# A graph network's tables in three bfloat16 parts: who casts and who subtracts between the neighbour sums

## The chip, the cores and the metric

The kernel runs on one core of a Trainium2 chip. A core has five engines with instruction streams of their own: TensorE (PE in the profile; its weight loads are PEld), VectorE (DVE), ScalarE (ACT), GpSimd (POOL) and SyncE (SP). They meet only through semaphores, and SP, ACT and POOL can also start DMA transfers. The metric is the device time of the whole program in microseconds (us), and lower is better.

## The reference

Four graph blocks run in sequence on 6250 nodes with 96 features and 200000 edges. The first is an attention layer, the second two layers with a maximum over neighbours, the third two layers with a mean (MEAN1, MEAN2 here), the fourth three graph convolutions (GCN1 to GCN3). Each block's result is added to its input and normalised. What the change touches are the sums over neighbours of the last two blocks:

```python
def _sage_layer(h, src, dst, W_l, b_l, W_r):
    msgs = h[src]
    agg = jax.ops.segment_sum(msgs, dst, num_segments=N_NODES)
    ...
    return mean @ W_l + b_l + h @ W_r
...
def gcn_conv(x, W, b, src, dst, deg_inv_sqrt):
    h = x @ W
    msgs = h[src] * norm[:, None]
    out = jax.ops.segment_sum(msgs, dst, num_segments=N)
    out = out + h * (deg_inv_sqrt * deg_inv_sqrt)[:, None]
    return out + b
```

## The kernel before

Nodes lie in 49 blocks of 128 partitions (NB), which are handled in 7 groups of 7 blocks (NG, GB). In the three earlier passes over the edges the kernel gathers rows edge by edge. In the second and third of these it also builds, in device memory, a matrix of counts: how many edges lead from each node to each other, as bfloat16. The five sums (n = 0 for MEAN1, 1 for MEAN2, 2 to 4 for GCN1 to GCN3) are then dense matrix products of this matrix with the table of the layer's rows.

The count matrix is read anew for each sum, in 49 blocks of 1568 KB. `load_blocks` (L413 to L430) loads each block in two halves of 784 KB: SP loads one, ACT the other, each from its own instruction stream. Three blocks fit in the buffer (CNT16 in BUF), so a block may be loaded as soon as the sum of the block three places earlier is done (`sums_ready`). SP has nothing else to do and reaches the next sum's loads as soon as there is room. ACT reaches them when it has done everything that stands ahead of them in its stream (L1121 to L1128): the node phase of that sum.

To keep float32 accuracy the table TBW (in TB) is split into three bfloat16 parts that stand side by side in PARTS (in CG): the first part is the table cast to bfloat16; the rest is the table minus the first part, and goes to EGW (in EG); the second part is the rest cast; the third is the rest minus the second part. TensorE's block sum (L719 to L741) makes 49 matrix products of a 128x128 piece of counts with 288 columns of PARTS, accumulated in one of three PSUM banks (psA, psB, psX), and VectorE takes each block from there (`take_block`, L1686 on). The first block of a sum waits at every seventh product for that group's parts (`parts_made`, L734).

Between two sums lies a node phase that makes the new table, group by group, over all engines:

- TensorE transposes 7 blocks of rows into psX (L671), and multiplies the transposed rows by the layer's weights into psO (L679). It transposes group g + 1 ahead of multiplying group g. psO holds one group, and is free again at `out_used`.
- ACT copies psX to XTQ (`rows_transposed`, L900), one copy per group. In MEAN2 it also copies the other half of psO to R (`root_rows`, L905, shown as ARENA) and gives psO back. In GCN1 to GCN3 VectorE gives it back.
- VectorE takes the table out of psO (`take_rows`: L1247 in MEAN2, L1244 in the GCNs, shown as TB), casts the first part (L1215) and subtracts (L1216), both in `split`, L1211.
- GpSimd casts the second part (L486) and subtracts for the third (L489), in the loop `second_and_third_parts` (L481), once for each sum.

Each engine's order is written out by hand; nothing is scheduled by a planner.

Of the kernel before, what the change touches and what calls it, by code (L numbers as in the profile page):

```python
# [8 lines left out]
DIM = 96  # L9
# [6 lines left out]
GB = 7  # L16
NG = NB // GB
# [44 lines left out]
ALU = mybir.AluOpType  # L62
# [4 lines left out]
ATT, PROJ, MAX1, MAX2, MEAN1, MEAN2, GCN1, GCN2, GCN3 = range(9)  # L67
PHASE_COLS = [W0 + HEADS, DIM] + [2 * DIM] * 4 + [DIM] * 3

PASS_OF_PHASE = {ATT: 0, MAX1: 1, MAX2: 2, MEAN1: 3, MEAN2: 4, GCN1: 5, GCN2: 6, GCN3: 7}  # L70
GATHER_PASSES = 3
MAX_PASSES = (1, 2)


EARLY, LATE = slice(0, NB - GB), slice(NB - GB, NB)
# [27 lines left out]
def build(nc, x, src, dst, dst_before, src_tiles, dst_tiles, edge_attr, att_W, att_src, att_dst, gat_bias, proj_WT, proj_b, ln_g, ln_b,  # L103
# [7 lines left out]
    def sem(name):  # L111
        return ctx.enter_context(nc.semaphore(name))
# [25 lines left out]
    TBW = TB[:, 0:NB * DIM].rearrange("p (b w) -> p b w", w=DIM)  # L138
    EG = sb("EG", [P, NB * W0])
    EG0 = EG[:, :].rearrange("p (b w) -> p b w", w=W0)  # L140
    EGW = EG[:, 0:NB * DIM].rearrange("p (b w) -> p b w", w=DIM)
# [34 lines left out]
    PARTS = CG[:, 0:NB * 3 * DIM // 2].bitcast(BF16).rearrange("p (b w) -> p b w", w=3 * DIM)  # L176
# [122 lines left out]
    table_made = sem("table_made")  # L299
# [54 lines left out]
    again_taken = sem("again_taken")  # L354
    again_step = sem("again_step")
    large_known = sem("large_known")
    rest_made = sem("rest_made")
    second_made = sem("second_made")
    parts_made = sem("parts_made")
# [75 lines left out]
    def _(pool):  # L435
# [12 lines left out]
        for b in range(NB):  # L448
            g, j = b // GB, b % GB
# [31 lines left out]
        def second_and_third_parts(n):  # L481
            with pool.Fori(0, NG) as g:
                here = bass.ds(g * GB, GB)
                pool.wait_ge(rest_made, g + (n * NG + 1))
                pool.sem_inc(turn["pool"], 1)
                nc.gpsimd.tensor_copy(PARTS[:, here, DIM:2 * DIM], EGW[:, here, :]).then_inc(second_made, 1)  # L486
                pool.wait_ge(second_made, g + (n * NG + 1))
                pool.sem_inc(turn["pool"], 1)
                nc.gpsimd.tensor_tensor(PARTS[:, here, 2 * DIM:3 * DIM], EGW[:, here, :], PARTS[:, here, DIM:2 * DIM],  # L489
                                        ALU.subtract).then_inc(parts_made, 1)  # L490
# [11 lines left out]
        for q in range(GATHER_PASSES):  # L502
# [10 lines left out]
            if q == 0:  # L513
                pool.wait_ge(step_row_stored, 16)
            if q in MAX_PASSES:
                for j in range(CS):
# [4 lines left out]
                    in_offset=bass.IndirectOffsetOnAxis(ap=last_i[:, b:b + 1], axis=0)).then_inc(end_gathered[b // GB], 16)  # L521

        second_and_third_parts(0)

        for n in range(1, 8 - GATHER_PASSES):
            second_and_third_parts(n)

    @block.sync
    def _(sp):
# [360 lines left out]
    def _(act):  # L890
# [11 lines left out]
        def root_rows(f, g):  # L902

            act.wait_ge(table_made, PASS_OF_PHASE[f] * NG + g + 1)
            nc.scalar.copy(R[:, g * GB:(g + 1) * GB, :], OUTG[:, :, DIM:2 * DIM]).then_inc(out_used, 1)  # L905

        def node_phase(f, first=0):

            for g in range(first, NG):
                rows_transposed(f, g)  # L910
                if g and f in (MAX1, MAX2, MEAN1, MEAN2):
                    root_rows(f, g - 1)
            if f in (MAX1, MAX2, MEAN1, MEAN2):
                root_rows(f, NG - 1)

        def attention_pass():

# [182 lines left out]
        for f in (MAX1, MAX2, MEAN1, MEAN2, GCN1, GCN2, GCN3):  # L1100
# [14 lines left out]
            else:  # L1115
                n = PASS_OF_PHASE[f] - GATHER_PASSES
# [16 lines left out]
    def _(dve):  # L1133
        steps = [0, 0]

        def link(ins, behind=0):


            steps[0] += 1
            ins.then_inc(dve_step, 1)  # L1140
            dve.wait_ge(dve_step, steps[1] + (steps[0] - behind))
# [7 lines left out]
        tt = nc.vector.tensor_tensor  # L1149
# [61 lines left out]
        def split(here, g):  # L1211


            rest = EGW[:, here, :]
            link(nc.vector.tensor_copy(PARTS[:, here, 0:DIM], TBW[:, here, :]))  # L1215
            link(tt(rest, TBW[:, here, :], PARTS[:, here, 0:DIM], ALU.subtract))  # L1216
            dve.sem_inc(rest_made, 1)  # L1217
# [20 lines left out]
        def take_rows(f, g):  # L1238

            here = slice(g * GB, (g + 1) * GB)  # L1240
            dve.wait_ge(out_ready, g + (out_group_base(f, "rows") + 1))
            if f in PASS_OF_PHASE:
                if f in (GCN1, GCN2, GCN3):
                    tt(TBW[:, here, :], OUTG[:, :, 0:DIM], dis[:, here].unsqueeze(2).broadcast_to([P, GB, DIM]),  # L1244
                       ALU.mult).then_inc(table_made, 1)
                else:
                    ts(TBW[:, here, :], OUTG[:, :, 0:DIM], 1.0, None, ALU.mult).then_inc(table_made, 1)  # L1247
                if f in (MAX1, MAX2):
                    return
                dve.wait_ge(table_made, g + (PASS_OF_PHASE[f] * NG + 1))  # L1250
                if f in (GCN1, GCN2, GCN3):
                    dve.sem_inc(out_used, 1)
                split(here, g)

        def node_rows(f):

            for g in range(NG):
                take_rows(f, g)
            rows_taken(f)

        def rows_taken(f):
            if f in PASS_OF_PHASE:
                dve.wait_ge(table_made, (PASS_OF_PHASE[f] + 1) * NG)
            dve.wait_ge(out_used, out_group_base(f, "rows") + NG + 1)
# [5 lines left out]
        for g in range(NG):  # L1270
            here = slice(g * GB, (g + 1) * GB)
# [515 lines left out]
        for g in range(NG):  # L1787
            here = slice(g * GB, (g + 1) * GB)
# [26 lines left out]
        for g in range(NG):  # L1815
            here = slice(g * GB, (g + 1) * GB)
# [82 lines left out]
```

## Time and profile before

| | us |
|---|---|
| median of 3 runs | 8144.81 |
| the runs | 8144.05 to 8150.12 |
| the profiled execution | 8149.13 |
| its span on the core | 8147.2 |

The profile is of one execution. The first 6811 us of the span are the attention and maximum layers and MEAN1. The rest is four stretches of one kind: a node phase, then 49 block sums of some 6 us. MEAN2's node phase begins at 6811 us, GCN1's at 7151, GCN2's at 7481 and GCN3's at 7811.

### The profile page before, as it was taken

What the parts mean: (1) busy time and instruction counts of PE and PEld (TensorE: products, weight loads), DVE (VectorE), ACT (ScalarE), POOL (GpSimd) and SP (SyncE); (2) the same over time, 40 slices, a digit from 0 to 9 for tenths busy, and PEclk for the clock granted to TensorE, in tenths of its full rate; (3) what the DMA queues carried; (4) which work ended last, traced back from release to release, by engine and by line L of the source; (5) the groups of instructions that cost most, each with busy time, mean ns of one, the idle gap of its engine ahead of it and who ended that gap; (6) DMA issues with size and microseconds to landing.
All of it is one profiled execution on the core that took longest, in us unless ns stands there. A gap on an engine that the chain in (4) does not pass through costs nothing.

```text
span 8147.2 us, 70764 instructions
## 1 busy us (share of the span) xinstructions
PE 4234.8 (52%) x19184; PEld 2471.1 (30%) x19184; DVE 5020.9 (62%) x9411; ACT 2884.7 (35%) x5375; POOL 4827.2 (59%) x5030
## 2 busy tenths in 40 slices
PE   2110000000255555666665566566566598999999
PEld 1000000000131111111113111111111398999999
DVE  4654444444568888888786778878887774222232
ACT  0222222222255555555553555555555300010000
POOL 6777777777637777777776777777777500000000
PEclk6555555555565555555555555555555599999999
DMA  5333333333224444444443444444444275766767
GB/s 132 88 98 85 85 87 87 85 85 85 66 86 131 130 131 133 132 131 133 133 131 101 133 131 131 133 133 131 131 133 132 84 268 199 267 223 220 267 228 248
DMA packets 642166, 1129.68 MB, mean 139 GB/s; under 512 B 164844, under 2 KB 422271, under 8 KB 641618
## 3 DMA queue, kind: packets, MB, share of 16 engines
q1 hardware_dynamic: 360112, 437.17, 17.2%
q0 software_dynamic: 159184, 251.10, 14.8%
q10 hardware_dynamic: 122578, 438.40, 13.6%
q14 instruction: 216, 1.77, 0.1%
q8 instruction: 76, 1.25, 0.1%
HBM read 713.46 MB, written 412.70 MB: 138 GB/s over the span
## 4 chain that ended last, share of the span: by engine, by line
POOL 48%; PE 21%; issue 17%; DVE 10%; DMA 4%; ACT 1%; DVEq 0%; POOLq 0%; SPq 0%; ACTq 0%
POOL CG L460 46%; PE psX L736 6%; PE psB L736 6%; PE psA L736 6%; DMA CG<-table,BUF 3%; DVE BUF L1550 2%; PE psO L679 1%; DVE XTQ L1576 1%; DVE BUF L1545 1%; DVE STG L1576 1%; DVE BUF L1542 1%; DVE XTQ L1569 1%; DVE STG L1569 1%; ACT X L1045 1%; POOL EG L519 1%
## 5 line engine op out<-in xcount | busy, mean ns | idle before, releaser
L460 POOL DMA_INDIRECT CG<-table,BUF x4704 | 4482.0, 953 | 1567.5 <-issue 1351.7
L706 PE MATMUL psO<-WE,BUF 128*128 128x384 f32 x1568 | 1141.7, 883 | 381.7 <-DMA BUF<-in_edge_attr 381.7
L1001 ACT ACTIVATE BUF<-iota,EG 128x128 bf16<-128x128 f16 x3136 | 958.0, 387 | 205.1 <-ACT CG L981 103.0
L779 PE MATMUL psA<-ident,F 128*100 128x128 f32 x1 | 0.5, 455 | 1704.3 <-DVEq L1451 1704.3
L486 POOL CAST CG<-EG x35 | 26.9, 769 | 1296.1 <-DVEq L1217 1296.1
L977 ACT COPY psX<-BUF 128x384 f32<-128x384 f32 x392 | 189.0, 482 | 1540.0 <-DVE XTQ L1576 771.0
L706 PEld LDWEIGHTS psO<-WE,BUF 128*128 128x128 f32 x1568 | 459.6, 323 | 893.8 <-DMA BUF<-in_edge_attr 646.5
L1542 DVE TENSOR_SCALAR BUF<-iota,EG 128x392 bf16<-128x392 f16 x1568 | 562.1, 358 | 46.9 <-DMA EG<-step_rows 19.1
L1480 DVE TENSOR_TENSOR terms<-CG,ARENA 128x64 f32<-128x64 f32 x98 | 26.3, 269 | 904.2 <-DMA CG<-table,BUF 903.7
L1545 DVE TENSOR_SCALAR BUF<-iota,EG 128x392 bf16<-128x392 f16 x1568 | 543.4, 347 | 6.5 <-PE psB L716 3.3
L779 PEld LDWEIGHTS psA<-ident,F 128*100 128x100 f32 x1 | 0.2, 162 | 1704.7 <-DVEq L1451 1704.7
L1569 DVE TENSOR_TENSOR XTQ<-CG,psO 128x768 f32<-128x768 f32 x196 | 288.2, 1470 | 366.6 <-DMA CG<-table,BUF 366.6
L736 PE MATMUL psA<-CG,BUF 128*128 128x288 bf16 x4018 | 509.3, 287 | 6.4 <-DMA BUF<-counts 6.1
L736 PE MATMUL psB<-CG,BUF 128*128 128x288 bf16 x4018 | 508.7, 287 | 7.2 <-DMA BUF<-counts 6.9
L1569 DVE TENSOR_TENSOR STG<-CG,psO 128x768 f32<-128x768 f32 x196 | 288.4, 1471 | 355.4 <-DMA CG<-table,BUF 355.4
L736 PE MATMUL psX<-CG,BUF 128*128 128x288 bf16 x3969 | 500.9, 286 | 0.5 <-POOL CG L489 0.5
L736 PEld LDWEIGHTS psB<-CG,BUF 128*128 128x128 bf16 x4018 | 494.8, 142 | 9.7 <-issue 7.2
L736 PEld LDWEIGHTS psA<-CG,BUF 128*128 128x128 bf16 x4018 | 494.9, 142 | 9.2 <-POOL CG L489 7.0
L736 PEld LDWEIGHTS psX<-CG,BUF 128*128 128x128 bf16 x3969 | 488.3, 142 | 1.6 <-POOL CG L489 0.8
L715 PE MATMUL psA<-BUF 128*128 128x392 bf16 x523 | 250.4, 479 | 405.1 <-DVE BUF L1545 396.3
L715 PE MATMUL psB<-BUF 128*128 128x392 bf16 x523 | 250.1, 478 | 401.8 <-DVE BUF L1545 393.0
L1005 ACT ACTIVATE BUF<-BUF,ones 128x1024 bf16<-128x1024 bf16 x392 | 449.7, 1147 | 12.7
(284 smaller groups left out, 7533.6 us busy)
## 6 DMA issues: line engine op xcount, KB each, us to landing
BUF<-counts SPq DMA_DIRECT2D x245, 784.0 KB, 5.8
BUF<-counts ACTq DMA_DIRECT2D x245, 784.0 KB, 6.4
counts<-BUF SPq DMA_DIRECT2D x1572, 98.0 KB, 2.3
hist<-CG ACTq DMA_DIRECT2D x392, 384.0 KB, 2.4
hist<-CG ACTq DMA_DIRECT2D x196, 416.0 KB, 2.5
CG<-table,BUF POOLq DMA_INDIRECT x4704, 2.5
BUF<-in_edge_attr SPq DMA_DIRECT2D x392, 128.0 KB, 3.3
table<-TB SPq DMA_DIRECT2D x14, 336.0 KB, 2.6
```

The source lines that it names most:

```text
L460: pool.indirect_dma_start(out=rows_in[:, u % RING, k, :], out_offset=None, in_=tab, in_offset=bass.IndirectOffsetOnAxis(ap=SRC[:, u * S + ...
L706: mm = pe.matmul(ETERM[:, s, a, 0:4 * DIM], EA[:, s, a, :], WE[:, m, :, :].rearrange("k c d -> k (c d)"), start=True, stop=True)
L715: pe.matmul(sums, LOW[:, s, j, 0, :], RHS[:, j, 0, :], start=True, stop=False)
L736: mm = pe.matmul(sums[:, 0:3 * DIM], CNT16[:, B % 3, b:b + NB * (P - 1) + 1:NB], PARTS[:, b, :], start=b == 0, stop=b == NB - 1, skip_grou ...
L977: nc.scalar.copy(reset_cols[:, :, 1:K9], reset[:, u * S:(u + 1) * S].unsqueeze(1).broadcast_to([P, DIM // 2, S])).then_inc(resets_ready, 1)
L1001: far = nc.scalar.activation(FAR[:, j, a, :], iota16[:, 0:P], ACT.Square, bias=STEP[:, 2 + a, u * CS + j:u * CS + j + 1], scale=-1.0)
L1005: nc.scalar.activation(LOW[:, u % 2, :, :, :], FAR, ACT.Relu, bias=ones[:, 0:1], scale=-1.0).then_inc(low_ready, 1)
L1542: ts(RHS[:, j, 0, :], iota16[:, :], STEP[:, 0, n:n + 1], None, ALU.is_equal)
L1545: ts(RHS[:, j, 1, :], iota16[:, :], STEP[:, 1, n:n + 1], None, ALU.is_equal).then_inc(onehot_ready, 1)
L1550: stt(ACC[:, j, :], ACC[:, (j - 1) % CS, :], STEP[:, 4, n:n + 1], step_sums[k % 3], ALU.mult, ALU.add).then_inc(acc_ready, 1)
L1569: tt(max_cols[b][:, :, 1:K9].rearrange("p c (a k) -> p c a k", a=2), ROWSW[:, r, :, :].rearrange("p (a k) c -> p c a k", a=2), ETERM[:, s, ...
L1576: scan = nc.vector.tensor_tensor_scan(out=columns, data0=reset_flat, data1=columns, initial=0.0, op0=ALU.add, op1=ALU.max)
```

## The change

In MEAN2, GCN1, GCN2 and GCN3 (`SPLIT_HERE`) ACT now makes the first and the second part, and VectorE both subtractions. ACT's new casts stand one and two groups behind its copies out of psX; VectorE's second subtraction stands one group behind its first. GpSimd's loop runs only for MEAN1, whose split stays as it was. A new semaphore, `first_made`, tells VectorE of a finished first part, and VectorE waits at the end of the node phase until all parts are made.

```diff
@@ -521,9 +523,6 @@
         second_and_third_parts(0)
-
-        for n in range(1, 8 - GATHER_PASSES):
-            second_and_third_parts(n)
@@ -910,8 +909,28 @@
                 rows_transposed(f, g)
                 if g and f in (MAX1, MAX2, MEAN1, MEAN2):
                     root_rows(f, g - 1)
+                if g and f in SPLIT_HERE:
+                    if g >= 2:
+                        second_part(f, g - 2)
+                    first_part(f, g - 1)
             if f in (MAX1, MAX2, MEAN1, MEAN2):
                 root_rows(f, NG - 1)
+            if f in SPLIT_HERE:
+                second_part(f, NG - 2)
+                first_part(f, NG - 1)
+                second_part(f, NG - 1)
+
+        def first_part(f, g):
+            here = slice(g * GB, (g + 1) * GB)
+            act.wait_ge(table_made, PASS_OF_PHASE[f] * NG + g + 1)
+            nc.scalar.copy(PARTS[:, here, 0:DIM], TBW[:, here, :]).then_inc(first_made, 1)
+
+        def second_part(f, g):
+            here = slice(g * GB, (g + 1) * GB)
+            act.wait_ge(rest_made, (PASS_OF_PHASE[f] - GATHER_PASSES) * NG + g + 1)
+            nc.scalar.copy(PARTS[:, here, DIM:2 * DIM], EGW[:, here, :]).then_inc(second_made, 1)
@@ -1250,12 +1269,34 @@
-                split(here, g)
+                if f in SPLIT_HERE:
+                    if g:
+                        third_part(f, g - 1)
+                    rest_of_first(f, g)
+                else:
+                    split(here, g)
+
+        def rest_of_first(f, g):
+            here = slice(g * GB, (g + 1) * GB)
+            dve.wait_ge(first_made, SPLIT_HERE.index(f) * NG + g + 1)
+            link(tt(EGW[:, here, :], TBW[:, here, :], PARTS[:, here, 0:DIM], ALU.subtract))
+            dve.sem_inc(rest_made, 1)
+
+        def third_part(f, g):
+            here = slice(g * GB, (g + 1) * GB)
+            dve.wait_ge(second_made, (PASS_OF_PHASE[f] - GATHER_PASSES) * NG + g + 1)
+            tt(PARTS[:, here, 2 * DIM:3 * DIM], EGW[:, here, :], PARTS[:, here, DIM:2 * DIM],
+               ALU.subtract).then_inc(parts_made, 1)
         def node_rows(f):
             for g in range(NG):
                 take_rows(f, g)
+            if f in SPLIT_HERE:
+                third_part(f, NG - 1)
+                dve.wait_ge(parts_made, (PASS_OF_PHASE[f] - GATHER_PASSES + 1) * NG)
             rows_taken(f)
```

ACT's stream from GCN2's node phase to its first load of counts reads so before (XTQ is the transposed rows; TENSOR_LOAD large reads the flag that picks the branch with the loads):

```order
L900 COPY XTQ<-psX 96x896 [waits transposed] x2
L900 COPY XTQ<-psX 96x896 [waits out_ready,transposed] x5
L1124 TENSOR_LOAD large
L1124 ISA x2
L1125 COMPARE_AND_BRANCH
L429 UNCONDITIONAL_BRANCH
L429 ISA
L426 ISA [waits sums_ready]
```

The same place in the changed kernel, from the last copy of transposed rows on (CG is PARTS, TB the table, EG the rest; line numbers are those of the changed kernel):

```order
L899 COPY XTQ<-psX 96x896 [waits out_ready,transposed]
L933 CAST CG<-EG 128x7x96 [waits rest_made]
L927 CAST CG<-TB 128x7x96 [waits table_made]
L933 CAST CG<-EG 128x7x96 [waits rest_made]
L927 CAST CG<-TB 128x7x96 [waits table_made]
L933 CAST CG<-EG 128x7x96 [waits rest_made]
L1143 TENSOR_LOAD large
L1143 ISA x2
L1144 COMPARE_AND_BRANCH
L431 UNCONDITIONAL_BRANCH
L431 ISA
L428 ISA [waits sums_ready]
```

Five casts, each with a wait on VectorE, stand now between ACT's last copy and its first load of counts.

VectorE's stream at the end of GCN2's node phase reads so before (the last group and the first block taken):

```order
L1244 TENSOR_TENSOR TB<-psO,dis 128x672 [waits dve_step,out_ready]
L1215 CAST CG<-TB 128x7x96 [waits table_made]
L1216 TENSOR_TENSOR EG<-TB,CG 128x672 [waits dve_step]
L1686 TENSOR_REDUCE EG<-psA 128x96 [waits dve_step,sums_ready,out_used,table_made]
L1676 TENSOR_TENSOR EG<-EG,TB 128x96 [waits sums_used]
```

And in the changed kernel:

```order
L1263 TENSOR_TENSOR TB<-psO,dis 128x672 [waits dve_step,out_ready]
L1290 TENSOR_TENSOR CG<-EG,CG 128x7x96 [waits table_made,second_made]
L1283 TENSOR_TENSOR EG<-TB,CG 128x672 [waits first_made]
L1290 TENSOR_TENSOR CG<-EG,CG 128x7x96 [waits dve_step,second_made]
L1727 TENSOR_REDUCE EG<-psA 128x96 [waits out_used,sums_ready,table_made,parts_made]
```

The cast is gone from VectorE's stream, and a second subtraction stands in it that waits for ACT.

## Rows read from the trace of the kernel before

**Rows 1.** Page, part 1: busy us (share of span) and instructions of each engine.

```profile
PE 4234.8 (52%) x19184; PEld 2471.1 (30%) x19184; DVE 5020.9 (62%) x9411; ACT 2884.7 (35%) x5375; POOL 4827.2 (59%) x5030
```

**Rows 2.** Windows, inside GCN2's sum: length; PE, PEld, DVE, ACT, POOL; clock, DMA, GB/s.

```profile
7527.00:7790.00 263.00, 263.00 (x2149) 263.00 (x2148) 54.71 (x176) 0.00 (x0) 0.00 (x0) 1.00 0.75 267
```

**Rows 3.** Chain that ended last, MEAN2's node phase to its sum: start, us, what.

```profile
6847.90 0.87 DVE TB L1247
6848.79 0.49 ACT ARENA L905
...
6849.31 0.18 ACTq L1124
...
6850.00 4.59 DMA BUF<-counts
```

**Rows 4.** Timeline, MEAN2: start, us, engine, line, operation [idle before <-releaser].

```profile
6842.80 0.72 ACT L905 COPY ARENA<-psO 128x672 f32<-128x672 f32 x1 [2.78 <-DVE TB L1247]
...
6854.72 7.66 PE L736 MATMUL psB<-CG,BUF 128*128 128x288 bf16 x49 [6.86 <-DMA BUF<-counts]
...
6862.22 6.17 PE L736 MATMUL psX<-CG,BUF 128*128 128x288 bf16 x49
```

**Rows 5.** Timeline of GCN2's node phase and the start of its sum.

```profile
7498.68 0.86 DVE L1216 TENSOR_TENSOR EG<-TB,CG 128x672 f32<-128x672 f32 x1
...
7499.69 0.86 DVE L1244 TENSOR_TENSOR TB<-psO,dis 128x672 f32<-128x672 f32 x1
...
7500.75 1.77 PE L679 MATMUL psO<-WR,XTQ 96*128 96x96 f32 x14 [0.36 <-DVEq L1252]
7500.96 1.46 POOL L489 TENSOR_TENSOR CG<-EG,CG  x1 [0.27 <-POOL CG L486]
7501.58 1.56 DVE L1216 TENSOR_TENSOR EG<-TB,CG 128x672 f32<-128x672 f32 x1
...
7503.28 0.86 DVE L1244 TENSOR_TENSOR TB<-psO,dis 128x672 f32<-128x672 f32 x1
...
7506.92 0.90 ACT L900 COPY XTQ<-psX 96x896 f32<-96x896 f32 x1 [2.69 <-PE psX L671]
...
7507.93 32.23 ACTq L426 DMA_DIRECT2D BUF<-counts  x7
...
7514.06 0.86 DVE L1244 TENSOR_TENSOR TB<-psO,dis 128x672 f32<-128x672 f32 x1
...
7521.37 6.17 PE L736 MATMUL psB<-CG,BUF 128*128 128x288 bf16 x49
```

**Rows 6.** Chain that ended last, end of GCN2's node phase: start, us, what.

```profile
7518.94 1.47 POOL CG L489
...
7520.45 1.08 PE psA L736 x7
```

**Rows 7.** Tile counts, ACT's first load of GCN2's sum (issued at 7507.93).

```profile
DMA to landing us min/median/max: 4.5/4.5/4.5
```

**Rows 8.** Timeline of GCN1: tables taken out of psO, second block's start.

```profile
7172.54 0.86 DVE L1244 TENSOR_TENSOR TB<-psO,dis 128x672 f32<-128x672 f32 x1
...
7183.52 0.86 DVE L1244 TENSOR_TENSOR TB<-psO,dis 128x672 f32<-128x672 f32 x1
...
7190.95 6.17 PE L736 MATMUL psA<-CG,BUF 128*128 128x288 bf16 x49
```

**Rows 9.** Timeline of GCN3: the same three places.

```profile
7824.24 0.86 DVE L1244 TENSOR_TENSOR TB<-psO,dis 128x672 f32<-128x672 f32 x1
...
7838.62 0.86 DVE L1244 TENSOR_TENSOR TB<-psO,dis 128x672 f32<-128x672 f32 x1
...
7845.93 6.17 PE L736 MATMUL psX<-CG,BUF 128*128 128x288 bf16 x49
```

**Rows 10.** Groups by line and form, ACT: count, busy us, mean ns, idle before them.

```profile
L981 ACT COPY CG<-STG 128x768 f32<-128x768 f32 x196 | 307.3, 1568 | 0.0
...
L905 ACT COPY ARENA<-psO 128x672 f32<-128x672 f32 x28 | 20.1, 717 | 83.2 <-DVE TB L1247 83.2
```

More of the change, by code:

```diff
@@ L72 @@
 MAX_PASSES = (1, 2)
+SPLIT_HERE = (MEAN2, GCN1, GCN2, GCN3)
 EARLY, LATE = slice(0, NB - GB), slice(NB - GB, NB)
@@ L356, in build @@
     large_known = sem("large_known")
+    first_made = sem("first_made")
     rest_made = sem("rest_made")
```

## The prediction

> **What bounds the kernel now.** I read the page first. GpSimd is busy for 59% of the span and VectorE for 62% [rows 1], but almost all of that lies in the first 6811 us, which the change doesn't touch. So I read the last 1336 us only, by windows. Inside a sum TensorE is busy for all of the 263 us of the window, at full clock, with DMA at 0.75 of its engines' time [rows 2]: the sums are TensorE's, a block in 6.0 us, and nothing that starts late is made up later, since TensorE has no idle time there to give back. What can change are the four node phases in between, from the last block of one sum to the second block of the next, where TensorE waits for others.
>
> Then I asked the chain of waits who ends a node phase. In MEAN2 it is not the split. The last table group is taken at 6847.90, ACT copies its half of psO, reads the flag, starts its first load of counts at 6850.00, and this transfer takes 4.59 us [rows 3]. TensorE had been idle for 6.86 us when it came [rows 4]. In GCN2 ACT's first load leaves at 7507.93, while the node phase still runs, and lands 4.5 us later [rows 5, 7], so at 7512.4, ahead of TensorE's first block. There the end is the split: VectorE's three operations per group, then GpSimd's subtraction, then the last seven products of block 0 [rows 6]. GCN1 and GCN3 look the same.
>
> **Part 1: VectorE is rid of a collision.** While GpSimd subtracts for 1.46 us (from 7500.96), VectorE's own subtraction takes 1.56 us instead of 0.86 [rows 5]. I checked the period of a GCN group: from one table taken to the next it is 7503.28 - 7499.69 = 3.59 us with the collision, 3.66 in GCN1, as (7183.52 - 7172.54)/3 [rows 5, 8]. Without it VectorE's three operations are 3 x 0.86 plus some 0.35 of gaps, 2.9 us; and the round through psO is the product's 1.77 us, the table's 0.86 and two handings over (the product started 0.2 us after the table was done, and TensorE's end reaches VectorE in about 0.2), 3.0 us. So a group costs 3.0 instead of 3.6. Until the third table nothing is gained: there the products are longer, and VectorE waits for them. From there to the last table: GCN2 has four periods, (7514.06 - 7499.69) - 12.0 = 2.4 us; GCN3 (7838.62 - 7824.24) - 12.0 = 2.4 us [rows 9]; GCN1 from the fourth table on has three, (7183.52 - 7172.54) - 9.0 = 2.0 us. In MEAN2 the product is longer, ACT sits idle for 2.78 us a group [rows 4] and its two new casts of about 0.6 us of occupancy each fit there: no gain, no loss.
>
> The Trainium skill weighs in on the size of this: the page "SBUF — State Buffer", section "Who interferes with whom", says that a VectorE operation with two SBUF inputs is held until a reading GpSimd operation has ended. By that rule the held subtraction would end 0.86 us after 7502.42, so at 7503.28; the trace ends it at 7503.14, and the row agrees within 0.14. The gain would be the same 0.7 us a group by either.
>
> **Part 2: the casts on ACT.** ACT gets 14 casts of 128x672 a phase. The trace of before has none from SBUF to bfloat16 of that form. The nearest row is L905, the same number of elements out of PSUM: 0.717 us [rows 10]. The far bound above is L981, which reads with a stride: 1568/768 = 2.04 ns an element, so 1.37 us for 672. I take 0.72, because the cast's inner runs are 96 contiguous elements on both sides, as L905's nearly are. A cheaper one than 0.6 I exclude, as its elements are no fewer.
>
> **Part 3: what is queued behind them.** This is the term that decides. ACT's first three loads of counts stand behind its last cast, and the last cast waits for VectorE. Let t be the start of the last table group. In a GCN: table done t + 0.86; first part of group 6 by ACT to t + 1.6; VectorE has meanwhile done the third part of group 5 (to t + 1.9), then the rest of group 6 to t + 2.75; with 0.15 for the semaphore the last cast starts at t + 2.9. From the start of a copy of this form to the DMA's issue MEAN2 shows 6850.00 - 6848.79 = 1.2 us [rows 3] (GCN2 1.0, from 7506.92 to 7507.93 [rows 5]). So the load leaves at t + 4.1 and TensorE starts block 0 after 4.6 + 0.1 us, at t + 8.8. Before, the load left 6.1 us ahead of t; that is a delay of 10 us for the load, of which the split's old tail covered a part.
>
> Block 0 then follows an idle TensorE. MEAN2's block 0, after 6.86 us of idling, took 6862.22 - 6854.72 = 7.5 us to the next block's start instead of 6.0 [rows 4]; I take this for all four. So the second block starts at t + 16.3.
>
> Before it started at t + 7.4 in GCN1 (7190.95 - 7183.52) and t + 7.3 in GCN2 and GCN3 (7521.37 - 7514.06; 7845.93 - 7838.62) [rows 5, 8, 9]. The loss is 8.9, 9.0 and 9.0 us; less the gain of part 1 it is 6.9, 6.6 and 6.6.
>
> In MEAN2 t doesn't move. ACT does its copy of psO from t + 0.9, the second part of group 5 from 1.5, the first of group 6 from 2.1 to 2.85; VectorE the third part of 5 from 2.25 to 3.1, the rest of 6 to 4.0; the last cast starts at t + 4.15, the load leaves at t + 5.35 instead of t + 2.1. Loss 3.25 us, and block 0 is as slow as it was.
>
> The Trainium skill has a rule against such an order, in "DMA: Bandwidth & Descriptors", section "Rules for kernel authors": issue a DMA early, compute, and wait late, so that its fixed cost lies under the work. The trace agrees on the cost of the other order (MEAN2's 6.86 us of waiting [rows 4]); by that rule each of the three GCN loads goes from hidden to paid.
>
> **Part 4: at nothing.** Splitting ends sooner (last third part at about t + 4.5, before 7520.4, t + 6.3), but that is now under the transfer, worth nothing. GpSimd's 56 operations leave a queue that nobody else used. VectorE's wait for all parts ends before the first block's sum comes. SP's halves are issued as before.
>
> **The sum:** 3.25 + 6.9 + 6.6 + 6.6 = 23.4 us slower. Against the profiled execution's 8149.1 that is 8172.5; the median of the runs is 4.3 us lower, so 8144.8 + 23.4 = 8168.2 us.
>
> **The rivals.**
>
> A: the load doesn't wait. If ACT's stream reached its DMA ahead of the casts' ends, or block 0 waited for something else, the loads would land as before and the split's tail would decide: block 0 would start when the last product ends, run into group 6's parts at t + 4.5, which is before it needs them, and only part 1's gain would count, 2.0 + 2.4 + 2.4 = 6.8 us faster: 8138, within 0.2% of before, so not slower. It decides at one point: in a GCN the load must have left by about t - 2, which it did at t - 6.1 before. Against it speaks MEAN2, where the load left 1.2 us after the last copy's start and TensorE waited for it. 6%.
>
> B: the casts are slow, at 1.37 us. Then ACT's 0.9 + 2 x 1.37 us make a GCN group 3.7 us, the gain of part 1 is gone (6.8 us), two casts on a GCN's tail add 1.3 us each phase and MEAN2 gets 2 us at the tail and 1 in its groups: 23.4 + 6.8 + 3.9 + 3 = 37, 8182. 8%.
>
> C: the clock stays low for longer after 8 to 10 us of idling than after MEAN2's 6.86. At the worst all of block 0 runs at half clock, 12.0 us instead of 7.5 in four phases: 8168 + 18 = 8186. 6%.
>
> D: the loads are late but cost less: the transfer lands sooner on a quiet machine, and the clock is back sooner (6.0 for block 0). 1.5 us in each GCN and 1 us of issue and landing in all four take 8.5 off: 8160, within 0.2%. 10%.
>
> **How the numbers follow.** My forecast, 8163 to 8174 around 8168, has 70%. A measurement of this kernel tells about 0.2% (16 us, so 8161.1) from no change. Slower: forecast, B, C, and nothing of D, 0.84, from which I take a little for errors on the low side: 0.82. Same: A, D and that little, 0.17. Faster by over 16 us has no mechanism: 0.01. The range leaves out A below and C above: 8156 to 8180, down past D and up to short of B.
>
> **What would show it.** In the trace after: ACT's first load of counts some 4 us behind the last table in GCN1 to GCN3, and 5.3 in MEAN2; TensorE idle for 8 to 9 us ahead of block 0, released by DMA of counts, not by the third part; VectorE's subtractions all at 0.86; a GCN group at 3.0 us; casts on ACT of 0.7 to 0.8. It is wrong if ACT's loads leave before the last cast, if the third part releases block 0, or if TensorE's blocks inside a sum are not 6.0 us.

## The result

| | before | after |
|---|---|---|
| median, us | 8148.05 | 8174.01 |
| runs, side by side on one chip | 8 (8144.05 to 8152.92) | 8 (8167.39 to 8176.02) |
| profiled execution, us | 8149.13 | 8174.0 |
| its span, us | 8147.2 | 8172.1 |

The ratio of after to before is 1.003, with a 95% interval of 1.0021 to 1.0039. The change costs 26.0 us; the prediction had 23.4.

The page's first part says little, as it said before [rows 1]: GpSimd has 58 us less to do, ACT 39 us more, and the program is longer.

```profile
PE 4226.2 (52%) x19184; PEld 2469.9 (30%) x19184; DVE 5009.8 (61%) x9411; ACT 2924.1 (36%) x5431; POOL 4769.2 (58%) x4974
```

The groups by line show the new operations. First ACT's casts from 6811 us on, for the rest and for the table (count | busy us, mean ns | idle ahead and what ended it); then VectorE's two subtractions from 7157 us on.

```profile
L933 ACT CAST CG<-EG 128x672 bf16<-128x672 f32 x28 | 21.1, 753 | 11.5 <-DVEq L1284 11.5
L927 ACT CAST CG<-TB 128x672 bf16<-128x672 f32 x28 | 21.1, 753 | 18.7 <-DVE TB L1263 18.7
...
L1290 DVE TENSOR_TENSOR CG<-EG,CG 128x672 bf16<-128x672 f32 x21 | 18.0, 857 | 5.3 <-ACT CG L933 2.6
L1283 DVE TENSOR_TENSOR EG<-TB,CG 128x672 f32<-128x672 f32 x21 | 17.9, 851 | 2.5 <-ACT CG L927 2.5
```

A cast takes 0.75 us, and no subtraction is stretched any more: their means are 0.85 us, where a stretched one took 1.56 [rows 5]. So each of the moved operations is cheap, and the loss is elsewhere. The chain that ended last, in MEAN2 (answering to [rows 3]), shows where:

```profile
6853.81 0.49 ACT CG L933
6854.33 0.18 ACTq L1143
...
6855.02 4.74 DMA BUF<-counts
...
6859.89 7.68 PE psB L735 x49
```

The last cast, then the reading of the flag, then the load, then block 0. The timeline of the same place (answering to [rows 4]):

```profile
6849.72 0.86 DVE L1266 TENSOR_SCALAR TB<-psO 128x672 f32<-128x672 f32 x1 [1.99 <-PE psO L678]
...
6859.89 7.68 PE L735 MATMUL psB<-CG,BUF 128*128 128x288 bf16 x49 [10.21 <-DMA BUF<-counts]
...
6867.41 4.82 PE L735 MATMUL psX<-CG,BUF 128*128 128x288 bf16 x38
```

TensorE idles 10.21 us ahead of block 0, where it idled 6.86 before. In GCN1 the wait is new (answering to [rows 8]):

```profile
7183.32 0.86 DVE L1263 TENSOR_TENSOR TB<-psO,dis 128x672 f32<-128x672 f32 x1 [0.24 <-PE psO L678]
...
7186.20 0.86 DVE L1263 TENSOR_TENSOR TB<-psO,dis 128x672 f32<-128x672 f32 x1 [0.24 <-PE psO L678]
...
7188.92 0.75 ACT L933 CAST CG<-EG 128x672 bf16<-128x672 f32 x1 [1.08 <-DVEq L1284]
...
7189.93 24.79 ACTq L428 DMA_DIRECT2D BUF<-counts  x6
...
7194.44 7.66 PE L735 MATMUL psX<-CG,BUF 128*128 128x288 bf16 x49 [8.28 <-DMA BUF<-counts]
...
7201.93 6.17 PE L735 MATMUL psA<-CG,BUF 128*128 128x288 bf16 x49
```

A group now takes 7186.20 - 7183.32 = 2.88 us, and everything after the last table is later. TensorE's waits from 6800 us on list all four places (sum in us, times, longest; psB stands for two of them):

```profile
PE psB L735 <- DMA BUF<-counts: 18.6, 2, 10.2
...
PE psA L735 <- DMA BUF<-counts: 8.5, 1, 8.5
...
PE psX L735 <- DMA BUF<-counts: 8.3, 1, 8.3
```

To compare kernels I use one measure, read off each timeline: a **phase** runs from the first transposes of a node phase to the start of the second block of its sum. The **last stretch** runs from MEAN2's first transposes to the end of the span.

| us | MEAN2 | GCN1 | GCN2 | GCN3 | sum | last stretch |
|---|---|---|---|---|---|---|
| before | 50.9 | 39.3 | 40.5 | 34.7 | 165.4 | 1335.9 |
| after | 54.3 | 44.6 | 50.5 | 38.6 | 187.9 | 1358.9 |
| difference | +3.4 | +5.3 | +10.0 | +3.9 | +22.6 | +23.0 |
| predicted | +3.25 | +6.9 | +6.6 | +6.6 | +23.4 | |

The phases hold nearly all of it. Another 1.8 us lie ahead of MEAN2 (its first transposes start at 6813.15 instead of 6811.32), where the change has no part. In e1 to e4 below that start lies anywhere from 6811.69 to 6816.19, so the 1.8 us may be mere scatter.

### The profile page after: what moved, and what is told of

Its sections match the earlier page's. It is cut to its first block, busy times and chain, and to the rows that moved or that the text cites. A ratio compares the mean times of both kernels' runs of the same rounds, so it can differ in the third digit from the quotient of the medians.

```text
span 8172.1 us, 70547 instructions
## 1 busy us (share of the span) xinstructions
PE 4226.2 (52%) x19184; PEld 2469.9 (30%) x19184; DVE 5009.8 (61%) x9411; ACT 2924.1 (36%) x5431; POOL 4769.2 (58%) x4974
## 3 DMA queue, kind: packets, MB, share of 16 engines
q1 hardware_dynamic: 360112, 437.17, 17.1%
## 4 chain that ended last, share of the span: by engine, by line
POOL 48%; PE 21%; issue 16%; DVE 9%; DMA 4%; ACT 1%; DVEq 0%; POOLq 0%; SPq 0%; ACTq 0%
POOL CG L462 46%; PE psX L735 6%; PE psB L735 6%; PE psA L735 6%; DMA CG<-table,BUF 3%; DVE BUF L1591 2%; PE psO L678 2%; DVE STG L1617 1%; DVE BUF L1586 1%; DVE XTQ L1617 1%; DVE BUF L1583 1%; DVE STG L1610 1%; DVE XTQ L1610 1%; POOL EG L454 1%; POOL EG L521 1%
## 5 line engine op out<-in xcount | busy, mean ns | idle before, releaser
L714 PE MATMUL psX<-BUF 128*128 128x392 bf16 x522 | 248.1, 475 | 394.8 <-DVE BUF L1586 394.7
```

What stands on the lines that cost most here:

```text
L714: pe.matmul(sums, LOW[:, s, j, 0, :], RHS[:, j, 0, :], start=True, stop=False)
```

## The experiments

Two questions are tested: is the loss the place of ACT's loads behind the casts, or something else that the change brought; and what is the move of the casts worth by itself. TensorE's clock became a third. I call TensorE, its products and its blocks *cold* where they ran at the lower of its two clock levels: the fourteen products of a GCN group take 1.70 to 1.77 us at the higher level and 3.14 at the lower.

### Loads ahead of the casts (e1)

The changed kernel, but ACT reads the flag and starts its loads of the first three blocks right behind its first copy out of psX. The edit, in ACT's node phase:

```diff
             for g in range(first, NG):
                 rows_transposed(f, g)
+                if g == first and f in (MEAN2, GCN1, GCN2, GCN3):
+                    flag = act.value_load(large[0:1, 0:1], min_val=0, max_val=1)
+                    with act.If(flag == 0):
+                        load_blocks(act, "act", PASS_OF_PHASE[f] - GATHER_PASSES, True, "first")
```

The loop that starts the loads now begins with the fourth block.

> The changed kernel, but in MEAN2 and the GCNs ACT reads the flag and starts the first three loads of counts right behind its first copy of transposed rows of the node phase, ahead of all its casts but the first; the loads of the other blocks stay where they were. Everything is computed. Theory (ACT's late loads cost the time): the waits of block 0 on DMA of counts (10.2, 8.3, 8.5 and 8.4 us in the changed kernel) go, block 0 is started when the last product ends and runs into group 6's parts, ready some 4.4 us after the last table in a GCN and 5.7 in MEAN2, so the second block starts 7.0 to 7.4 us after the last table (15.7 to 17.7 in the changed kernel). Against before: MEAN2 6.9 us less, since before waited for its load too, GCNs 2.5 to 3 us less each by a period of 2.87 instead of 3.6: about 8148 - 16 = 8132. Rival (the casts' longer round between ACT and VectorE, or ACT's extra work, is what costs): the time stays near the changed kernel's 8174, and block 0 is released by the third part.

Measured: 8138.92 us (8136.14 to 8142.9, 11 runs) against 8152.79 for before on the same chip (24 runs): ratio 0.9982, interval 0.9973 to 0.9991. Phases 43.3, 38.5, 39.0 and 33.2, sum 154.0, which is 33.9 less than after. The timeline of its GCN2:

```profile
7480.62 1.31 ACTq L428 DMA_DIRECT2D BUF<-counts  x3
...
7506.44 6.17 PE L739 MATMUL psA<-CG,BUF 128*128 128x288 bf16 x49
7506.64 0.86 DVE L1271 TENSOR_TENSOR TB<-psO,dis 128x672 f32<-128x672 f32 x1 [0.24 <-PE psO L682]
...
7510.15 0.86 DVE L1298 TENSOR_TENSOR CG<-EG,CG 128x672 bf16<-128x672 f32 x1 [0.88 <-ACT CG L941]
...
7512.44 3.84 PE L739 MATMUL psB<-CG,BUF 128*128 128x288 bf16 x30
```

The loads leave 26 us ahead of the last table, TensorE goes from its last product straight into block 0, and the second block starts 5.8 us behind the last table (7512.44 - 7506.64) instead of 16.95. In GCN1 and GCN3 it is 7.5 and 7.4 us, since their last product (3.27 us) and block 0 (7.7 us) were cold. No wait of TensorE on the counts is left. The cause of the loss is gone, and the changed kernel's casts, with the loads in another place, are faster than both. Against before it gains 13.9 us where I had expected 16.

### Loads early in the kernel before (e2)

The same edit in the kernel before, with the split as it was.

> The kernel before, with ACT's first three loads of a sum moved ahead in the same way and nothing else. Theory: only MEAN2's load was late before (6.86 us), so it alone gains, the GCNs stay: 8148 - 7 = 8141, within 0.2% of before. The difference of this run to the run of the casts with early loads is then what the casts' move is worth by itself, some 9 us. Rival (loads never mattered): 8148.

Measured: 8144.83 us (8140.42 to 8150.43), ratio 0.9991, interval 0.9982 to 1.0: -8.0 us, with an interval that just reaches no change. The phases are 43.0, 40.1, 41.2 and 34.7. All of the gain is MEAN2's, -7.9; the three GCNs together move by +1.5, no more than they differ between kernels for the clock of their first groups (below). MEAN2's timeline:

```profile
6847.99 5.31 PE L740 MATMUL psB<-CG,BUF 128*128 128x288 bf16 x42
6848.19 0.86 DVE L1255 TENSOR_SCALAR TB<-psO 128x672 f32<-128x672 f32 x1 [3.35 <-PE psO L683]
...
6853.77 1.08 PE L740 MATMUL psB<-CG,BUF 128*128 128x288 bf16 x7 [0.47 <-POOL CG L493]
```

Block 0 starts with its first 42 products at once and waits only for the third part of the last group. So the fault that the change spread to the GCNs stood in MEAN2 before.

### Loads late in the kernel before (e3)

The kernel before, with one wait ahead of ACT's reading of the flag. Nothing is cast elsewhere; ACT is only held until GpSimd has made all second parts.

```diff
                 else:
+                    act.wait_ge(second_made, (n + 1) * NG)
                     flag = act.value_load(large[0:1, 0:1], min_val=0, max_val=1)
```

> The kernel before, with one wait added: from MEAN2 on ACT waits for GpSimd's last cast of the node phase ahead of reading the flag and starting its loads. No cast is moved. Theory: the load leaves 0.7 us after that cast's end, t + 4.5 in MEAN2 and about t + 5.3 in a GCN (t is the start of the last table), instead of t + 2.1 and t - 6.1; block 0 starts 4.7 us later and takes 7.5. MEAN2 loses 2.4 us, a GCN 17.5 - 7.3 = 10.2: 8148 + 33 = 8181, slower than the changed kernel even though the casts are where they were. Rival (the casts cost it): 8148, no change.

Measured: 8189.17 us (8182.4 to 8196.1, 5 runs), ratio 1.0043, interval 1.003 to 1.0057: +36.4 us, expected +33. The phases are 54.0, 51.0, 51.8 and 44.5. GCN2:

```profile
7533.37 0.86 DVE L1245 TENSOR_TENSOR TB<-psO,dis 128x672 f32<-128x672 f32 x1 [0.32 <-PE psO L679]
...
7537.04 0.74 POOL L486 CAST CG<-EG  x1 [1.12 <-DVEq L1218]
...
7538.82 13.81 ACTq L426 DMA_DIRECT2D BUF<-counts  x4
...
7543.39 8.62 PE L736 MATMUL psA<-CG,BUF 128*128 128x288 bf16 x49 [10.06 <-DMA BUF<-counts]
...
7551.85 4.33 PE L736 MATMUL psB<-CG,BUF 128*128 128x288 bf16 x34
```

The load leaves 5.45 us behind the last table, and the same wait as in after appears, 10 us long, in a kernel whose casts haven't moved. That settles the first question: the place of the load in ACT's stream is enough for the loss. The four kernels make a square: from before's 165.4 us, early loads give 159.0, the moved casts with early loads 154.0, late loads without moved casts 201.3, and the moved casts with the loads behind them 187.9. The two late kernels are not late alike, though: in a GCN the load leaves 5.5 to 5.7 us behind the last table in e3 and 3.7 in after.

### MEAN2 as before (e4)

The changed kernel with `SPLIT_HERE = (GCN1, GCN2, GCN3)`, and GpSimd's loop run for MEAN1 and MEAN2.

> The changed kernel with MEAN2 split as before (VectorE casts the first part, GpSimd makes the second and third), the GCNs as changed. Theory: ACT's load in MEAN2 leaves at t + 2.1 again instead of t + 5.3, so the phase gets its 3.3 us back and the time is 8174 - 3.3 = 8171. Rival (part of MEAN2's loss is not the load's place in the stream): less than 3.3 us come back between MEAN2's first transposes and its second block.

Measured: 8173.8 us (8167.33 to 8178.3, 8 runs), ratio 1.0025, interval 1.0014 to 1.0036: +21.0 us against before, where after had +26.0. MEAN2's phase is 51.0, 3.2 back of the 3.4 lost. Its timeline:

```profile
6852.76 0.86 DVE L1267 TENSOR_SCALAR TB<-psO 128x672 f32<-128x672 f32 x1 [3.35 <-PE psO L679]
...
6854.87 1.67 ACTq L428 DMA_DIRECT2D BUF<-counts  x3
...
6859.87 2.35 PE L736 MATMUL psB<-CG,BUF 128*128 128x288 bf16 x9 [7.15 <-DMA BUF<-counts]
```

The load leaves 2.11 us behind the table, as before. The term of MEAN2 stands by itself. The three GCNs, whose code is that of after, came out at 46.9, 45.6 and 40.2 instead of 44.6, 50.5 and 38.6: two of them differ by 2 us and one by 5, with the same loads and the same casts. Block 0 took 8.9, 7.9 and 8.7 us here. That scatter is what the next runs are about.

### Unread products ahead of block 0 (e5)

In all runs from here on, what lies ahead of MEAN2 took about 1.1 ms longer in every kernel (the kernel before, run beside them, took 9244, 9250 and 9274 us), for a reason that I don't know. Their times scattered over 0.9 to 1.6%, where those of the runs above kept within 0.2%. So these runs are read by their phases, and their ratios are only given beside. A phase has one profiled execution behind it.

The window of block 0 in after's GCN2, first to second block (columns as in [rows 2]):

```profile
7533.70:7542.20 8.50, 8.50 (x49) 6.92 (x50) 0.00 (x0) 0.00 (x0) 0.00 (x0) 0.70 0.33 137
```

The granted clock is 0.70 there: TensorE, after 8.48 us of idling, works a good part of block 0 at the lower of its two levels (1.2 GHz), and DMA has room. In MEAN2 it is 7.50 us at 0.79 and in GCN3 7.60 at 0.78: time times clock is 5.9 us in each, a block's length at full clock. e5 is the changed kernel with 60 products that nobody reads between the last product and block 0 of each of the four sums:

```diff
+FILL = 60
...
+            if n:
+                for _ in range(FILL):
+                    pe.matmul(psA[:, 0:3 * DIM], ones16[:, :], SEL16[:, 0:3 * DIM], start=True, stop=True,
+                              skip_group_check=True)
             for j in range(3):
                 sum_block(0, j, j == 0)
```

> The changed kernel, and TensorE makes 60 products of 128x128 by 288 columns that nobody reads, between the last product of a node phase and block 0 of the sum, in MEAN2 and the GCNs: 7.2 us at 0.12 us each, under the 8.3 to 10.2 us for which it waits there for the load. Theory of the second term (the idle wait before block 0 is paid twice, since block 0 then runs at the lower clock): from block 0's to block 1's start it takes 6.0 to 6.5 us instead of 7.49 to 8.51, so about 1.5 us less in each phase, 8174 - 6 = 8168. The waits on the load stay. Rival (block 0 is slow for another reason, such as its own transfers): it stays at 7.5 us and more.

Measured: 9252.79 us against 9244.01, ratio 1.0008 (0.9979 to 1.0038). Phases 53.8, 44.5, 42.6 and 40.9, sum 181.7. The same window in its GCN2:

```profile
8613.10:8619.10 6.00, 6.00 (x52) 6.00 (x51) 0.00 (x0) 0.00 (x0) 0.00 (x0) 1.00 0.37 153
```

And the timeline:

```profile
8604.09 0.86 DVE L1268 TENSOR_TENSOR TB<-psO,dis 128x672 f32<-128x672 f32 x1 [1.70 <-PE psO L679]
...
8613.08 6.17 PE L736 MATMUL psA<-CG,BUF 128*128 128x288 bf16 x49
8619.09 3.10 PE L736 MATMUL psB<-CG,BUF 128*128 128x288 bf16 x24
```

In all three GCNs block 0 takes 6.01 to 6.04 us at clock 1.00, though the load is as late as in after. So the extra 1.5 to 2.5 us of block 0 are the clock's: idle time is paid once as a wait and once more as a slow block behind it. In MEAN2 it took 7.60, at clock 0.79: there the unread products ended 2.5 us ahead of the load's landing. In GCN1 they ended 1.7 us ahead of it, and block 0 still took 6.04. In GCN2 and GCN3 they were partly cold themselves, took 9.4 and 9.7 us instead of GCN1's 7.5, and overran the load. So it started at t + 9.0 to 9.3 instead of 8.2 to 8.4 (t is the start of the last table, as in the prediction). The filler is no remedy for a late load; it measures what the clock takes. That the sum of the phases is 6 us below after's, as expected, is luck: GCN2's alone is 7.9 shorter, of which block 0 is 2.5, and most of the rest lies ahead of the last table, where e5 changes nothing; GCN3's is 2.3 longer.

### Both remedies together (e6, e9, e12)

e1 with 8 unread products (`fill(8)`) behind the first transposes of each node phase, and 7 ahead of each group's products in MEAN2 but the first, and ahead of the last group's in each GCN:

```diff
             transpose_group(0)
+            if f in SPLIT_HERE:
+                fill(8)
             for g in range(NG):
                 if g + 1 < NG:
                     transpose_group(g + 1)
+                if f == MEAN2 and g or f in SPLIT_HERE and g == NG - 1:
+                    fill(7)
                 multiply_group(g)
```

> The changed kernel with ACT's first three loads early, and short unread products on TensorE in the node phases of MEAN2 and the GCNs: 8 behind the first transposes, 7 (0.85 us at full clock) ahead of each group's product in MEAN2, and 7 ahead of the last in a GCN. Theory (with the loads gone the node phase is paced by TensorE's clock, which falls in its idle gaps): the last group's period falls from 4.4 to 2.9 us in the GCNs and from 6.0 to 4.3 in MEAN2, block 0 takes 6.2 instead of 7.0 to 7.8, together 2 to 3 us a phase: 8139 - 10 = 8129. Rival: the unread products only add their own time, 8139 or more.

Measured: 9207.22 us, ratio 0.9962 (0.9935 to 0.999). Phases 39.1, 33.1, 27.6 and 28.0, sum 127.7: 26 us less than e1, not the 10 expected. GCN2:

```profile
8551.95 1.70 PE L687 MATMUL psO<-WR,XTQ 96*128 96x96 f32 x14
...
8567.84 1.02 PE L669 MATMUL psA<-SEL,ones 128*128 128x288 bf16 x7
...
8569.10 1.77 PE L687 MATMUL psO<-WR,XTQ 96*128 96x96 f32 x14 [0.24 <-DVEq L1288]
8570.71 6.17 PE L748 MATMUL psA<-CG,BUF 128*128 128x288 bf16 x49
...
8576.72 3.47 PE L748 MATMUL psB<-CG,BUF 128*128 128x288 bf16 x27
```

The first group's products take 1.70 us. In e1 the first three groups' took 3.14 each, and the first two groups 4.4 us each instead of 2.87. The granted clock of the whole node phase, up to block 0, shows the same, first for e1's GCN2, then for e6's:

```profile
7473.40:7506.40 33.00, 25.39 (x147) 24.00 (x148) 14.14 (x17) 14.08 (x18) 0.00 (x0) 0.69 0.25 96
```

```profile
8549.10:8570.70 21.60, 19.66 (x162) 17.66 (x163) 14.25 (x18) 14.08 (x18) 0.00 (x0) 1.00 0.40 148
```

I had counted the unread products on the last group and on block 0 and not seen that the first groups of a phase are cold as well. From the first group's products to the last's that is 5.2 us in GCN2 (22.4 in e1, 17.15 in e6), and 1.5 us more in the cold first transposes. The other 4.7 of its 11.4 us are an idle time of TensorE inside the first transposes that the profile puts down to nothing ("issue"); before has it in GCN2 too (4.5 us), and e6 has none. The unread products aren't needed for it to go: e5, which has none inside its phases, has no such idle time in GCN2's first transposes either, but one of 2.26 us inside the first group's products. In all nine profiles with such an idle time in GCN2 (before, after, e1 to e5, e7 and e10) one packet of a DMA queue of the kind "instruction" starts in it, 2.2 to 2.5 us before it ends. In after it is this one, between 7494.4 and 7494.5 us (packets, MB, share of the DMA engines); the idle time ends at 7496.77:

```profile
q8 instruction: 1, 0.02, 59.2%
```

So TensorE seems to wait there for its code. That is argued and not shown: other phases, e6's GCN2 among them, have such a packet without an idle time, and no run moves the code alone.

Since the size surprised me, the kernel was run twice more.

> The changed kernel with early loads and unread products once more, beside the same with the casts of before. Theory: the four phases took 127.7 us in the first run's trace, 165.4 in the kernel before; 8148 - 37 = 8111, some 0.45% faster than before. Rival: the short phases of that trace were chance of the clock, and it is 8139 as with early loads alone.

> The changed kernel with ACT's early loads and unread products, a third time, for its ratio to the kernel before. Theory: four phases of 128 to 132 us, ratio 0.9955 where the kernel before takes 8150 us. Rival: 0.998, as with early loads alone.

Phases of e9: 40.4, 36.3, 27.6 and 27.7, sum 132.0; ratio 0.9974 (0.9948 to 0.9999). Phases of e12: 39.4, 33.5, 27.6 and 27.8, sum 128.1; ratio 0.9973 (0.9947 to 0.9999). The phases repeat within 1.3 us but for GCN1's (33 or 36), where the clock was not held: its first group's products took 3.14 us in e6 and e12, its third and fourth group's in e9. The last stretch is 1298.2 us in e12 against 1335.9 in the kernel before: 38 us. If that held where the kernel before takes 8148 us, it would be 0.46%; no run measured that. Against the kernel run beside it e12 gained 0.27%, with an interval from 0.01 to 0.53%, which tells neither the expected 0.45% nor the rival's 0.2% to be wrong.

### The same in the kernel before (e8)

e2 with the same unread products, to price the casts' move where neither loads nor clock hide it.

> The kernel before (GpSimd casts and subtracts) with ACT's first three loads early and the same unread products on TensorE as in the kernel with changed casts, early loads and such products. Theory: with TensorE's clock kept up, VectorE's period of 3.6 us bounds a GCN group here, and 2.87 us there; the GCN phases are 5 to 8 us longer each than the 27.6 to 33.1 us measured there, MEAN2 equal at 39: some 18 us more in all, about 8148 - 18 = 8130. Rival (who casts is worth nothing once the loads are early): the two kernels come within 3 us of each other.

Measured: 9228.76 us against 9250.24, ratio 0.998 (0.9959 to 1.0001). Phases 40.2, 39.2, 32.7 and 32.7, sum 144.8. VectorE in GCN2:

```profile
8622.14 0.86 DVE L1261 TENSOR_TENSOR TB<-psO,dis 128x672 f32<-128x672 f32 x1
...
8624.03 1.56 DVE L1233 TENSOR_TENSOR EG<-TB,CG 128x672 f32<-128x672 f32 x1
...
8625.73 0.86 DVE L1261 TENSOR_TENSOR TB<-psO,dis 128x672 f32<-128x672 f32 x1
```

With GpSimd subtracting, VectorE's subtraction is stretched to 1.56 us and a group takes 3.59, in five of GCN2's six steps from table to table. With the moved casts all six take 2.87 in e6. That is 0.72 us times 5, 3.6 us. Another 1.5 us lie behind the last table: the split's tail is shorter, and the second block starts at t + 5.8 instead of 7.3. The phases say the same, 5.1 us: 32.7 against 27.6 in GCN2, and 32.7 against 27.7 to 28.0 in GCN3. In all, the move is worth 144.8 - 132.0 = 12.8 to 144.8 - 127.7 = 17.1 us, where I had expected 18. With the clock left to itself (e2 against e1) it is only 4.9: cold products hide VectorE's time in the first groups, and in GCN1 and GCN3 a cold last product and block 0 hide the shorter tail.

### Loads from the idle queue (e7, e10, e11)

The changed kernel, but SP, which has nothing else to do, starts both halves of the first three blocks, and ACT only loads from the fourth block on.

```diff
+        if part == "both":
+            for j in range(3):
+                load(0, j)
+                load(0, j, slice(BLOCK // 2, BLOCK))
```

> The changed kernel, ACT's casts and their order untouched, but from MEAN2 on SP starts both halves of the first three blocks of a sum, and ACT only the loads from the fourth block on. Theory (what costs is the load's place in ACT's stream, not ACT's work): block 0 no longer waits for a load, and the time is that of the kernel with early loads on ACT, 8139 within 4 us. Rival (ACT's 14 casts a phase, or TensorE's clock, hold the phase up by themselves): over 8150.

> The changed kernel where SP starts both halves of the first three blocks, once more, on the chip of the others. Theory as before: 8139 within 4 us, block 0 started 0.2 us ahead of the last table. Rival: over 8150.

Measured: e7 9242.74 us, ratio 0.999 (0.9957 to 1.0024), phases 40.3, 36.0, 36.4 and 33.5, sum 146.2. e10 9235.44 us, ratio 0.999 (0.997 to 1.001), phases 40.1, 35.7, 36.3 and 33.3, sum 145.4. GCN2 of e7:

```profile
8597.66 6.17 PE L739 MATMUL psA<-CG,BUF 128*128 128x288 bf16 x49
8597.86 0.86 DVE L1267 TENSOR_TENSOR TB<-psO,dis 128x672 f32<-128x672 f32 x1 [0.24 <-PE psO L682]
...
8603.67 1.51 PE L739 MATMUL psB<-CG,BUF 128*128 128x288 bf16 x11
```

Block 0 starts 0.2 us ahead of the last table, as in e1. So it doesn't matter which queue takes the loads, if nothing that waits stands ahead of them. The sum is 8 us below e1's, both times: here the last groups of MEAN2 and GCN1 and the second and third of GCN2 were at the higher clock or nearly so, in e1 they were cold. Why is open. The times can't show it; their ratios are not clear of 1.

With the unread products as well:

> The changed kernel with SP starting both halves of a sum's first three blocks and unread products on TensorE in the node phases. Theory: both measures act as in their own runs, the four phases take 128 to 132 us instead of 165 in the kernel before, so it is 33 to 37 us faster than the kernel before, whatever the rest of the program takes. Rival: who starts the loads matters once the clock is kept up, and it differs from the run with ACT's early loads by over 5 us.

Measured: 9256.75 us against 9274.37, ratio 0.9972 (0.9948 to 0.9996), phases 39.1, 30.0, 29.0 and 27.6, sum 125.6, last stretch 1299.4. The medians differ by 17.6 us and not by the 33 to 37 that I had expected; the last stretch is 36.5 us shorter than in the kernel before. Once the clock is held, the two places for the loads give nearly the same last stretch (e12: 1298.2).

## Why the prediction was right

The direction and the mechanism held, step by step (t is the start of the last table):

| step | predicted | measured in after |
|---|---|---|
| a cast | 0.72 us | 0.753 us |
| last cast, GCN / MEAN2 | t + 2.9 / 4.15 | t + 2.7 / 4.1 |
| load leaves | t + 4.1 / 5.35 | t + 3.7 / 5.3 |
| block 0 starts, GCN | t + 8.8 | t + 8.2, 8.4, 8.4 |
| block 0 takes | 7.5 us | 7.5 (MEAN2), 7.5, 8.5, 7.7 |
| second block, GCN | t + 16.3 | t + 15.7, 16.95, 16.1 |
| second block, MEAN2 | 3.25 later | 3.4 later |
| a GCN group | 3.0 us | 2.87 us |

**The collision (part 1).** It is gone as forecast: the subtractions fall from 1.56 to 0.85 us, and e8 shows 1.56 again. The Trainium skill, "SBUF — State Buffer", section "Who interferes with whom", has it that a VectorE instruction with two inputs in SBUF contends with a GpSimd instruction that reads SBUF; the trace agrees, with 1.56 us beside GpSimd's subtraction and 0.85 without. But the gain up to t was badly sized: I had 2.0, 2.4 and 2.4 us for the GCNs, and from a phase's first transposes to its last table the change was -3.0, **+0.4** and -4.8. In GCN1 that is a group's 2.87 us instead of my 3.0, and 0.5 us ahead of the first table. In the other two the step that failed is that I let the first products be as long in after as in before, and the last one as short. They follow the clock. GCN2's last product and table, and GCN3's first product (3.14 us before):

```profile
7521.94 3.28 PE L678 MATMUL psO<-WR,XTQ 96*128 96x96 f32 x14 [1.10 <-DVEq L1271]
...
7525.26 0.86 DVE L1263 TENSOR_TENSOR TB<-psO,dis 128x672 f32<-128x672 f32 x1 [1.74 <-PE psO L678]
...
7834.94 1.70 PE L678 MATMUL psO<-WR,XTQ 96*128 96x96 f32 x14
```

The last product of GCN2 took 3.28 us instead of 1.80, because the clock had fallen by then (0.67 granted from 7520 to 7525.2 us, after 1.00 from 7512 to 7520), for a reason that no run isolates; GCN3's first took 1.70 instead of 3.14. Against my figures GCN1 gained 1.0 us more, GCN2 2.8 less and GCN3 2.4 more. That these nearly cancel in the sum is luck.

**The casts (part 2).** The near row was the right one, 0.75 us against 0.72; rival B, with 1.37 us, fell.

**The load behind the casts (part 3).** This is the term that decided, and it is shown from three sides: e1 takes it away and the loss is gone, e3 makes it alone and the loss is there, and the wait on the counts stands in the list of waits in after and in none of e1's. Each GCN's load leaves 9.8 to 10.1 us later than before; I had 10. What decides is the issuing engine's own waits that stand ahead of the issue. The Trainium skill's rule in "DMA: Bandwidth & Descriptors", section "Rules for kernel authors", is to issue a DMA early and wait on its semaphore late; e1 and e2 agree with it by 33.9 and 6.4 us of phase time.

**Block 0 (part 3).** 7.5 us, taken from the one row that followed 6.86 us of idling, held for MEAN2 and GCN1 and was 1.0 short in GCN2. Rival C was in the right direction for that phase, with 1.0 us of its 4.5. After 7 to 11 us of idling it took 7.3 to 8.9 us in after, e3 and e4; in e5's GCNs, with 1.7 us of idling or none, 6.0.

**Nothing else (part 4).** The last third part was never waited for.

**Rivals.** A fell, since the load waited; its figure of 8138 is nevertheless e1's time (8138.92), by the edit that makes its condition true. That agreement is chance: A had 6.8 us less than before, and e1 has 13.9 less than the kernel run beside it (8152.79). It also gains in MEAN2 what A left out, and loses some to the clock in the GCNs. D had 0.4 us a phase of its mechanism, the issue at t + 3.7 instead of 4.1.

The median came out at 8174.0, 6 us above the forecast. Of these, 3.2 lie in the kernel before itself (8148.05 in these runs, 8144.81 in those that I had); the other 2.6 are the change's 26.0 us against 23.4, and the phases don't show them (22.6).

## What to carry to other kernels

When work is moved to an engine, read what stands behind it in that engine's stream, above all the start of a transfer: here 14 casts a phase at 0.75 us each were nearly free, and the transfers queued behind the last of them made the kernel 26 us slower. Start transfers ahead of anything that waits (e1: the same casts then made the kernel faster than before, ratio 0.9982, 0.9973 to 0.9991), or from a queue that has nothing to wait for (e7, shown by the phases alone). An idle time of TensorE ahead of a long burst is to be priced with its clock: here the wait itself, 7 to 11 us, and 1.3 to 2.9 us more in the block that followed.

## What the hardware showed unexpectedly

TensorE's clock moved the phases about as much as the change did (22.6 us). Products of 1.70 us became 3.14 in the first groups of most phases. Code that was the same in after and in e4 gave GCN2 50.5 us in one and 45.6 in the other. Seven or eight unread products, a burst of 1.0 to 1.14 us at two places of a GCN phase, went with a granted clock of 1.00 through GCN2, and GCN3's products were at full clock from the first; some of GCN1's stayed cold. The sum of the four phases went from 154.0 to some 129 us, a bigger step than the moved casts and the early loads together (165.4 to 154.0). Up to 4.7 of these 25 us are the idle time without a releaser inside GCN2's first transposes (4.5 to 4.7 us in before, after and e1, none in e6). Why e7 and e10 kept the clock in groups where e1 didn't isn't settled.
